# The last stage of a graph layer with a mixture of experts: sums of squares on ScalarE, spare products on TensorE

## The reference

```
y = x + moe                                # x: the normed rows that entered the layer
mu = jnp.mean(y, axis=-1, keepdims=True)
var = jnp.var(y, axis=-1, keepdims=True)
out = xin + (y - mu) / jnp.sqrt(var + EPS) * gamma + beta
```

## Time and profile before

| | us |
|---|---|
| median of 3 runs | 467.93 |
| lowest and highest | 465.33, 468.48 |
| span of the profiled execution | 466.4 |
| last stage, first load issued to the end | 419.57 to 466.4 |
| mean granted TensorE clock | 0.883 |

### The profile page before, as it was taken

The page is one execution under the profiler, slowest core; times in us unless marked ns, Lnnn a source line. Parts: engine busy times, 40 slices in busy tenths (PEclk is TensorE's granted clock), DMA queues, the critical chain, the costliest instruction groups (busy, mean ns, idle before and its releaser), DMA issues.

```text
span 466.4 us, 11731 instructions
## 1 busy us (share of the span) xinstructions
PE 341.8 (73%) x2259; PEld 282.4 (61%) x2259; DVE 304.0 (65%) x1456; ACT 221.8 (48%) x592; POOL 311.9 (67%) x346
## 2 busy tenths in 40 slices
PE   2787798978798826300799999888898899806991
PEld 1576677867797725200687777777777778702330
DVE  3989897986979948430366666666555555601985
ACT  2578798888889643300233334333333334501441
POOL 6642777777777777673177777777777777760565
PEclk9999998997979965555799999999999999955997
DMA  6912345544645632296867777778777776318983
GB/s 182 325 70 98 114 166 160 174 157 165 187 153 189 224 131 102 103 252 201 220 185 205 210 222 218 220 218 220 216 225 206 231 223 173 82 34 318 334 294 136
DMA packets 61962, 87.97 MB, mean 189 GB/s; under 512 B 10503, under 2 KB 41149, under 8 KB 61780
## 3 DMA queue, kind: packets, MB, share of 16 engines
q1 hardware_dynamic: 32660, 44.89, 33.7%
q0 software_dynamic: 10720, 25.32, 15.2%
q10 hardware_dynamic: 18528, 17.19, 12.4%
HBM read 55.61 MB, written 32.73 MB: 189 GB/s over the span
## 4 chain that ended last, share of the span: by engine, by line
PE 26%; ACTq 16%; DVE 15%; issue 13%; DMA 9%; ACT 9%; SPq 6%; POOL 3%; DVEq 1%; POOLq 0%
PE psum L1187 7%; ACTq L564 6%; ACTq L277 5%; PE psum L1176 5%; ACTq L276 5%; ACT hid L569 4%; DMA sorted_x<-xrow,rows 3%; PE psum L1092 3%; DMA out_dram<-z 2%; PE psum L1110 2%; DVE z L1016 2%; DMA w_sb<-w_dram 2%; ACT xn L520 2%; DVE xmid L729 1%; POOL sorted_x L414 1%
## 5 line engine op out<-in xcount | busy, mean ns | idle before, releaser
L436 POOL DMA_INDIRECT token_y<-yb,xb x143 | 143.4, 1002 | 60.2 <-issue 38.7
L414 POOL DMA_INDIRECT sorted_x<-xrow,rows x128 | 123.4, 964 | 41.7 <-issue 39.1
L569 ACT ACTIVATE hid<-psum,b_sb 128x256 f32<-128x256 f32 (+1 forms) x188 | 69.3, 419 | 140.2 <-PE psum L1176 60.0
L1187 PE MATMUL psum<-w_sb,hid 128*128 x572 | 83.2, 283 | 12.0 <-ACT hid L569 11.9
L1187 PEld LDWEIGHTS psum<-w_sb,hid 128*128 128x128 f32 x572 | 74.5, 191 | 22.0 <-issue 19.3
L1176 PE MATMUL psum<-xbT,w_sb 128*128 128x256 f32 (+1 forms) x376 | 81.9, 341 | 2.1 <-DVE xbT L966 1.9
L975 DVE TENSOR_TENSOR yb<-psum,b_bc 128x256 f32<-128x256 f32 x94 | 33.9, 360 | 62.8 <-PE psum L1187 51.2
L1176 PEld LDWEIGHTS psum<-xbT,w_sb 128*128 128x128 f32 x376 | 57.6, 193 | 7.6 <-DVE xbT L966 4.2
L1166 PE MATMUL psum<-ident_aug,xb 128*128 128x128 f32 x143 | 33.3, 290 | 23.2 <-DMA xb<-sorted_x 21.2
L980 DVE SCALAR_TENSOR_TENSOR yb<-yb,xb 128x128 f32<-128x128 f32 x143 | 46.5, 353 | 3.3
L966 DVE COPY xbT<-psum 128x256 f32<-128x256 f32 x94 | 33.2, 353 | 23.6 <-PE psum L1166 23.5
(11 more groups left out here) (163 smaller groups left out, 559.4 us busy)
## 6 DMA issues: line engine op xcount, KB each, us to landing
xb<-sorted_x SPq DMA_DIRECT2D x49, 258.0 KB
w_sb<-w_dram ACTq DMA_DIRECT2D x83, 128.0 KB
adj_in<-adj_dram SPq DMA_DIRECT2D x32, 256.0 KB
got<-token_y SPq DMA_DIRECT2D x16, 512.0 KB, 5.9
xb<-sorted_x SPq DMA_DIRECT2D x45, 129.0 KB
out_dram<-z ACTq DMA_DIRECT2D x16, 256.0 KB, 3.2
w_sb<-w_dram SPq DMA_DIRECT2D x27, 128.0 KB
xmid<-x_dram SPq DMA_DIRECT2D x6, 512.0 KB, 8.1
```

The lines of the kernel that those rows point to most:

```text
L414: pool.indirect_dma_start(sorted_x, bass.IndirectOffsetOnAxis(ap=rows[:, slot, t, k:k + 1], axis=0), xrow[:, slot, k, t, :], None).then_in ...
L436: pool.indirect_dma_start(token_y, bass.IndirectOffsetOnAxis(ap=xb[:, q, t, TO:TO + 1].bitcast(I32), axis=0), yb[:, h, t, :], None, bounds ...
L569: last = act.activation(hid[:, u % RING, c, 0:n], psum[:, 2 + u % 2, c * BT:c * BT + n], ACT.Relu, bias=b1_sb[:, c, e])
L1187: last = mm(psum[:, 4 + u % 2, t * D:(t + 1) * D], hid[:, u % RING, c, t * P:(t + 1) * P], w2_sb[:, e, c * D:(c + 1) * D].rearrange("p a c ...
```

## The change

ScalarE now squares each tile of a group by itself, with the sum over its 128 columns written by the same call (`accum_out`) into a spare PSUM bank, and the root reads the sums there. VectorE's `add_squares` is gone, and its loop only scales. `squares` holds two tiles, and each square waits for the one two before it; the root waits, from the fifth group on, for the scaling of the group four before. On TensorE 14 products of the identity with stored expert weights go into a bank that nobody reads: as many as a unit has tiles each time that the scatter of one of the last eight units has landed, and two more before the first `add_pair`.

```diff
-        squares = sb("squares", [P, 2, GT, D])
-        rs3 = sb("rs3", [P, CRING, 3, GT])
+        squares = sb("squares", [P, 2, D])
+        rs3 = sb("rs3", [P, CRING, 2, GT])
+        sums_v = psum[:, CBANKS + 2, 0:CRING * GT].rearrange("p (q t) -> p q t", t=GT)
+        hold_ps = psum[:, CBANKS + 3, :]
...
             def square(g):
                 act.wait_ge(summed, g + 1)
-                if g >= 2:
-                    act.wait_ge(square_sums, g - 1)
-                act.activation(squares[:, g % 2, :, :].rearrange("p t c -> p (t c)"), psum[:, g % CBANKS, :], ACT.Square
-                               ).then_inc(squared, 1)
+                for t in range(GT):
+                    n = g * GT + t
+                    if n >= 2:
+                        act.wait_ge(square_sums, n - 1)
+                    act.activation(squares[:, t % 2, :], psum[:, g % CBANKS, t * D:(t + 1) * D], ACT.Square,
+                                   accum_out=sums_v[:, g % CRING, t:t + 1]).then_inc(square_sums, 1)
 
             def deviation(g):
                 q = g % CRING
-                act.wait_ge(square_sums, g + 1)
-                act.activation(rs3[:, q, 1, :], rs3[:, q, 0, :], ACT.Sqrt, bias=eps_t[:, :], scale=1.0 / D).then_inc(std_done, 1)
+                act.wait_ge(square_sums, (g + 1) * GT)
+                if g >= CRING:
+                    act.wait_ge(z_done, g - CRING + 1)
+                act.activation(rs3[:, q, 0, :], sums_v[:, q, :], ACT.Sqrt, bias=eps_t[:, :], scale=1.0 / D).then_inc(std_done, 1)
...
-            def add_squares(g):
-                dve.wait_ge(squared, g + 1)
-                if g >= CRING:
-                    dve.wait_ge(std_done, g - CRING + 1)
-                v.tensor_reduce(rs3[:, g % CRING, 0, :], squares[:, g % 2, :, :], axis=AX, op=ALU.add).then_inc(square_sums, 1)
-
...
-                n = step(v.reciprocal(rs3[:, q, 2, :], rs3[:, q, 1, :]))
+                n = step(v.reciprocal(rs3[:, q, 1, :], rs3[:, q, 0, :]))
...
-            for g in range(GROUPS + 1):
-                if g < GROUPS:
-                    add_squares(g)
-                if g:
-                    scale(g - 1)
+            for g in range(GROUPS):
+                scale(g)
...
+            def hold_clock(n):
+
+                for _ in range(n):
+                    mm(hold_ps, ident[:, :], w2_sb[:, 0:2, :].rearrange("p e c -> p (e c)"), start=True, stop=True)
+
+            for u in range(UNITS - OUT_RING, UNITS):
+                pe.wait_ge(yb_out[u % OUT_RING], 16 * sent(u, OUT_RING))
+                hold_clock(tiles_of(u))
+            hold_clock(2)
             for g in range(GROUPS):
                 add_pair(g)
```

## The result

The changed kernel takes 464.16 us (median of 17 runs, 461.74 to 466.81) against 467.07 (17 runs, 464.96 to 469.66). The ratio is 0.9935, 95% interval 0.9915 to 0.9954: 3.0 us less, 2.1 to 4.0, inside 1%. The profiled execution took 463.07 with a span of 461.3, so 1.8 lies around the span there; a second profiled execution of the kernel before took 467.84 with a span of 466.1, so 1.7. Two executions timed for the experiments, 1106 us of the kernel before and 471 us of the sums alone, ran far longer than their like and are left out throughout.

What follows compares the result with a forecast made beforehand. The last stage was taken as bound by a cold TensorE, then transfers holding z's slots, then VectorE. z(0) 2.8 us earlier, slots at 2.15 a group and the drain put z(15) 3.0 earlier: 464.9 from the median 467.93, range 462.4 to 471.0.

Steps and rivals of the forecast that it cites:

- the slots: Middle of the last stage: four slots of z, each freed when its store lands, pace it at 2.15 us a group.
- the cold clock: Start of the last stage: TensorE's low clock makes the first two pairs take 6.62 us, against 3.44 at the high level.
- z(0): Start of VectorE's scaling of the first group, z(g) that of group g: 428.5 for 431.34, 2.8 us earlier.
- z(15): Start of the last group's scaling, the end of the compared stage: 457.3 for 460.32.
- Spare products: Wait before the last stage: 14 products hold TensorE's clock, first square at 425.05 for 427.06.
- The cover: Time between the end of the spare products behind the last tile (422.0) and the first pair (423.24): 1.2 us.
- The squares: On ScalarE: four squares with sums a group, 0.36 us each, 1.75 with the root.
- The drain: From z(9) on: two groups at 1.24, four at 1.75 and 0.3 for late stores, reaching z(15) at 457.3.
- ScalarE as the bound: First rival: fetched sums cost up to 2.55 us a group, deciding from 2.19; up to 5.8 slower; chance 0.20.
- The second rival: Start of the last stage: spare products don't keep the clock, z(0) 0.5 us later than now, 467.7; chance 0.15.
- the free slots: Third rival: stores land beside loads as fast as alone (2.1 us), z every 1.75, 5.6 earlier, 462.4; chance 0.10.

Runs made afterwards that it cites:

- the sums alone: The changed kernel without the 14 spare products, timed against the kernel before: ratio 0.9968, stage 34.9 us.
- all rows of the table: The changed kernel and the follow-up runs, timed against the kernel before; their stages are compared with its one profiled stage of 37.1 us.
- the three other cold runs: Runs without spare products: changed kernel with four slots (0.9968), changed kernel with eight slots (0.9916), kernel before with eight slots (0.9959).

## Why the prediction was right, step by step

The forecast was 3.0 us less by way of a stage that starts 2.8 earlier, a middle paced by the slots, and a drain at TensorE's pace. The order of limits is confirmed by taking each away: the cold clock (3.3 alone), the slots (2.2 on top of the change), the sums (1.1 with four slots, 1.7 with eight). The sizes, from the first pair's start:

| | predicted | measured | before |
|---|---|---|---|
| first square | 1.8 | 2.0 | 3.8 |
| z(0) | 5.3 | 5.2 | 8.1 |
| z(4) | 13.5 | 12.9 | 16.3 |
| z(9) | 24.3 | 23.3 | 26.6 |
| z(15) | 34.1 | 32.7 | 37.1 |

*Spare products.* Right: the clock held, in all six profiled runs with 14 of them, through gaps of some 1.0 between them, and nothing waited for them. The cover was 0.5, not 1.2:

```profile
417.50 4.56 PE L1218 MATMUL psum<-w_sb,ident_aug 128*128 128x512 f32 x10 [1.01 <-DMA token_y<-yb,xb]
422.55 1.13 PE L1212 MATMUL psum<-got,ident_aug 128*128 128x512 f32 x2 [0.50 <-DMA got<-token_y]
```

They ended at 422.06, which is 3.5 behind the last tile's landing at 418.60, where I had three products, 2.6. Five stand in that row, two records each: the unit before has two tiles, its two products began at 417.50 and last 1.72, so they were still running when the last tile landed 1.1 later. The load took 3.74 from its issue, no less than before (3.63).

*The squares.* Mis-sized. I took 0.36 a tile and 1.75 a group; it is 0.25 and 1.25. I had added the whole of a one-column instruction to the square's spacing; the fetch overlaps the square and adds, against the copy's spacing, some 0.09. The Trainium skill ("ScalarE: Activation LUTs", section "What ACT_TABLE_LOAD costs") gives an activation with immediate scale and bias 186 ns and 0.833 a column, and an overlap of about 93 with its neighbour; by estimate from these figures a square without a sum stands 0.20 from the next. In the rows the fetch starts 0.17 to 0.20 after its square and the next square 0.05 after the fetch, so the trace is nearer to the Trainium skill's figure than to the copy's 0.15. The error of 0.5 a group hardly reached the end, because TensorE's 1.72 stood behind. That z(0) came out right is luck: the two groups of squares were 1.0 too long in my sum, but it had square 1 follow square 0 at once, though it put the end of the second pair later than that. In the trace square 1 waited 0.8 for that pair (426.29), and the first square came 0.2 later than I had it.

*The slots.* Right in kind, 0.6 too slow to z(4) and 0.4 from z(4) to z(9): the first stores landed after 5.0 to 5.2 and not 5.67, and the rate was 2.08, not 2.15. My reason for the slower rate, loads standing denser beside the stores, was wrong: the stores issued from 430 to 440 landed after 5.0 to 6.2, those of before from 433 to 444 after 5.6 to 6.5.

*The drain.* 9.4 for 9.8. VectorE waits for the root there, and the root, through the square before it, for TensorE's pair. I had put ScalarE's 1.75 a hair ahead of TensorE's 1.72; ScalarE has 1.25.

The sum is 1.4 too small for the profiled pair of runs, and right for the medians. Much of the difference seems to lie in which runs were profiled. Every timed run has a span: 465.5 in the middle of 53 runs of the kernel before, 461.8 in the middle of 17 of the changed one. That is 3.7 apart (3.1 by the means), where the two profiled pairs are 5.1 and 4.7 apart: both profiles of before (466.4 and 466.1) lie above the middle of its runs, both of the changed kernel (461.3 and 461.4) below. The offset of about 1.1 that all rows of the table share says the same. Beside the span lie 1.7 to 1.8 in all 53 runs of before, but 2.2 to 2.7 in four of the 17 of the changed kernel; what that is stays open. A cold start of 5.1 to 5.9 in most runs of before, instead of the 6.6 and 6.8 of its profiles, would make up about the 1.1; the three other cold runs suggest it, but nothing here profiles enough runs of before to show it. So the 3.0 hits partly by luck: two errors, a stage gain too small and a base run too long, lie opposite.

*The rivals.* ScalarE as the bound exists, beyond reach of this change. The second rival's price was too high: its case, the squares split and the pairs cold, is the run of the sums alone, which took 1.5 less than before by its ratio, where I had 0.2. With ten spare products the clock fell too, and the time stayed, since they used up most of the cold time themselves. For the free slots, the price of 5.6 less was for a ring that doesn't brake; with eight slots it was 6.6 by the stage and 5.4 by the ratio, so this was the gain that the change left lying.

## What to carry to other kernels

Before an engine is relieved, ask what it waits for once it is faster: here the store of four groups before, and that wait grew to 5.2 us, from 2.1 in the same list before. Count a ring by the longest landing that its transfers have beside others, not by the one they have alone; four more slots were worth more than the work saved (2.2 and 1.1 by the stage). Part of the space for them came out of the change itself, which made the buffer of squares 3 KB a partition smaller, where four slots take 8.

A start behind a long wait for transfers can be priced by its first instructions at both clock levels, and spare products in the wait bought the difference here, where they ended before the data came.

## What the runs showed of the hardware

- A sum with an activation is a second instruction (0.17 to 0.23 long), yet square and fetch of 128 columns stand only 0.25 apart, and the records of later ones in a row grow (0.28 to 0.33 in a group of four) while their spacing stays.
- The price of a cold start varies: the same two pairs, after 16 to 17 us without products, took 6.6, 6.8, 5.9, 5.7 and 5.1 in five profiled runs, against 3.7 with the clock held.
- A store of 256 KB landed after 2.1 us alone and 5.0 to 7.7 beside loads, where all transfers together moved 385 to 400 GB/s.
